# Attention and mixture block on one core: first stores on two queues, early projections in other banks, 69 unused products on TensorE

## The reference

```python
x = x + tanh(g_xattn[0]) * attention(layernorm(x), ctx_512)      # x: 8 x 256 x 128, ctx: 8 x 256 x 64
x = x + tanh(g_ffn[0]) * experts(layernorm(x))
# attention(x, c), 16 heads of 8 numbers
q, k, v = x @ Wq + bq, x @ Wk + bk, x @ Wv + bv
y = softmax(causal(q k^T / sqrt(8))) @ v
qc, kc, vc = x @ Wcq + bcq, c @ Wck + bck, c @ Wcv + bcv
y = y + softmax(qc kc^T / sqrt(8)) @ vc
return y @ Wp + bp
# experts(x): 16 experts of width 64, 2 of 4 groups and 4 experts chosen for each token
out = sum_e combine[:, e] * ((silu(x @ w_gate[e].T) * (x @ w_up[e].T)) @ w_down[e].T)
```

## Time and profile before

| | us |
|---|---|
| median of 3 runs | 352.14 (351.76 to 352.70) |
| the profiled execution, its own time | 352.36 |
| its span, first to last instruction | 350.6 |

### The profile page before, as it was taken

The page is one execution under the profiler, slowest core; times in us unless marked ns, Lnnn a source line. Parts: engine busy times, 40 slices in busy tenths (PEclk is TensorE's granted clock), DMA queues, the critical chain, the costliest instruction groups (busy, mean ns, idle before and its releaser), DMA issues.

```text
span 350.6 us, 8629 instructions
## 1 busy us (share of the span) xinstructions
PE 324.8 (93%) x3186; PEld 250.0 (71%) x3186; DVE 255.3 (73%) x639; ACT 196.1 (56%) x399; POOL 151.6 (43%) x174
## 2 busy tenths in 40 slices
PE   2577899999999999899999999999999999996896
PEld 1343474576687788678888789777978887774765
DVE  3325784777887888988889888787889965658642
ACT  2332244757876875586567656675756656542041
POOL 4783315203470169427743725286400461714222
PEclk9999999999999999999999999999999999999899
DMA  4547677577637686268647852366434203214000
GB/s 122 98 120 185 156 185 140 153 195 160 220 92 175 121 155 151 70 146 160 142 112 128 195 135 69 85 127 161 120 83 103 39 17 89 38 50 87 11 6 15
DMA packets 32890, 40.45 MB, mean 115 GB/s; under 512 B 3441, under 2 KB 29825, under 8 KB 30369
## 3 DMA queue, kind: packets, MB, share of 16 engines
q1 hardware_dynamic: 32848, 39.91, 49.6%
HBM read 29.84 MB, written 7.45 MB: 106 GB/s over the span
## 4 chain that ended last, share of the span: by engine, by line
PE 82%; DVE 7%; issue 2%; DMA 2%; ACT 2%; POOL 2%; SPq 2%; DVEq 0%; POOLq 0%; ACTq 0%
PE bank L891 15%; PE bank L825 15%; PE bank L782 9%; PE bank L804 8%; PE bank L779 7%; PE bank L912 7%; PE bank L801 6%; PE bank L845 3%; DVE row_max L978 2%; PE bank L866 2%; PE bank L831 2%; PE bank L861 1%; PE bank L925 1%; PE bank L852 1%; PE bank L847 1%
## 5 line engine op out<-in xcount | busy, mean ns | idle before, releaser
L978 DVE TENSOR_REDUCE row_max<-bank 128x2 f32<-128x512 f32 (+1 forms) x224 | 147.3, 686 | 45.5 <-PE bank L782 29.7
L694 ACT ACTIVATE probs<-bank 128x512 f32<-128x512 f32 x224 | 126.4, 595 | 55.3 <-PE bank L804 30.4
L891 PE MATMUL bank<-xn2T,w_pairs_sb 128*128 128x256 f32 x256 | 67.3, 387 | 1.2 <-DVE f_gate L1058 0.6
L825 PE MATMUL bank<-probs,v_ext 128*32 128x256 f32 (+1 forms) x1024 | 56.8, 363 | 0.0
L618 POOL TENSOR_TENSOR f_h<-f_h,comb 128x512 f32<-128x512 f32 x32 | 40.2, 1270 | 33.9 <-DMA comb<-c_scr 14.3
L782 PE MATMUL bank<-k_stack,q_stack 72*128 72x256 bf16 x256 | 50.8, 295 | 3.5 <-DMA k_stack<-k_scr 2.1
L891 PEld LDWEIGHTS bank<-xn2T,w_pairs_sb 128*128 128x128 f32 x256 | 43.7, 190 | 8.2 <-issue 3.1
L804 PE MATMUL bank<-q_stack,k_stack 73*128 73x256 bf16 x256 | 46.5, 285 | 0.2
L825 PEld LDWEIGHTS bank<-probs,v_ext 128*32 128x32 f32 x1024 | 29.8, 111 | 20.0 <-issue 3.4
L407 POOL TENSOR_TENSOR rest<-proj,part 128x512 f32<-128x512 f32 x14 | 16.2, 1159 | 54.7 <-ACT part L667 54.7
L779 PE MATMUL bank<-k_stack,q_stack 121*128 121x128 bf16 (+1 forms) x384 | 38.7, 231 | 0.3 <-DVE row_max L978 0.2
(11 more groups left out here) (113 smaller groups left out, 388.6 us busy)
## 6 DMA issues: line engine op xcount, KB each, us to landing
q_stack<-q_scr SPq DMA_DIRECT2D x15, 576.0 KB
k_stack<-k_scr SPq DMA_DIRECT2D x45, 192.0 KB
comb<-c_scr SPq DMA_DIRECT2D x14, 512.0 KB, 7.1
q_scr<-part SPq DMA_DIRECT2D x48, 64.0 KB
k_scr<-part SPq DMA_DIRECT2D x48, 64.0 KB
x_in<-in_x SPq DMA_DIRECT2D x8, 128.0 KB, 2.5
w_pairs_sb<-in_w_pairs SPq DMA_DIRECT2D x1, 1024.0 KB, 5.2
out<-y_out SPq DMA_DIRECT2D x8, 128.0 KB, 1.9
```

The source lines that it names most:

```text
L694: nc.scalar.activation(probs[:, seq % NP, :], exp_bank[s % 2][:, :], ACT.Exp).then_inc(exp_done, 1)
L825: last = pe.matmul(pv_bank[32 * n:32 * n + VW, col + q0:col + T], v[:, VW // 2 * odd:VW // 2 * odd + VW], weights, start=odd == 0 and kt = ...
L891: last = pe.matmul(bank_of[:, n * T:(n + 1) * T], w[:, e0:e0 + 128], xn2T[:, :], start=True, stop=True)
L978: nc.vector.tensor_reduce(row_max[:, kind, qt, h0:h0 + nh], max_bank[k % 2][:, :].rearrange("p (h k) -> p h k", h=nh), AX.X, ALU.max).then ...
```

## The change

**Stores and loads of element 0.** The functions `store_part`, `load_rows`, `load_stack` and `load_first` take the engine as an argument, and ACT issues five of the words that SP issued: `pd0:0`, `pd0:0:1`, `qh:0`, `qh:0:1` and `qst:0:1`. Each part has its own semaphore `part_out[kind][n]`, which counts two DMAs of an element.

**Projections of elements 0 to 2** (`EARLY = 3`) go to `gate_bank` (cross) and `up_bank` (self) instead of `misc`, with semaphores of their own. The first gates and ups wait until the last of them is copied out.

**`keep_busy`**: a product of the identity with itself, float32, 128 by 128, into `pv_bank`, whose result nothing reads. It waits for nothing, and PE's list has the word `warm:0` for it 69 times, all of them ahead of `exp:0:5`: 13 after `vproj:0`, 6 after `xnT:1`, 19 ahead of `max:0`, and 31 between the chunks `max:0` to `max:0:22`.

**`vclear`** clears the two halves of `v_ext` in two words, and waits for the cross parts of element 0 instead of for its normalised x.

**All five orders are written anew.** Other words than those named are the same, in another order; the first 60 or so of each engine differ most.

```diff
+EARLY = 3
+MISC_USES = [word for word in order("pe") if word[0] in MISC and not (word[0] == "proj" and word[1] < EARLY)]
...
-        part_out = [sem("part_out_cross"), sem("part_out_self")]
+        part_out = [[sem(f"part{n}_out_{kind}") for n in range(PARTS)] for kind in ("cross", "self")]
...
+        def store_part(eng, b, kind, n):
+            eng.wait_ge(split[kind], b * PARTS + n + 1)
+            if n == 0:
+                stack_here(eng, b - 2, kind)
+            q, k = part[:, kind, n, 0:T], part[:, kind, n, T:2 * T]
+            eng.dma_start(q_scr[b % 2, kind, n].rearrange("d h x -> (d h) x"), q).then_inc(part_out[kind][n], 16)
+            eng.dma_start(k_scr[b % 2, kind, :, n], k).then_inc(part_out[kind][n], 16)
...
+        def load_first(eng, qk, half):
+            for n in range(PARTS):
+                eng.wait_ge(part_out[CROSS][n], 32)
+            heads = slice(half * H // 2, (half + 1) * H // 2)
+            load_rows(eng, qk, 0, CROSS, heads, stack_in[0][CROSS] if half else first_heads_in)
...
-            def clear_values():
-                pool.wait_ge(xn_done, 1)
-                v = v_ext[:, :, :, :, :, :].rearrange("p a k n e v -> p (a k n) e v")
+            def clear_values(parity):
+                pool.wait_ge(split[CROSS], PARTS)
+                v = v_ext[:, parity].rearrange("p k n e v -> p (k n) e v")
...
             def project(b, kind):
-                misc_filled(act, "proj", b, kind)
+                src, done = (misc, misc_free) if b >= EARLY else ((gate_bank, up_bank)[kind], proj_free[kind])
+                if b < EARLY:
+                    act.wait_ge(proj_ready[kind], b + 1)
+                else:
+                    misc_filled(act, "proj", b, kind)
...
             def values(b):
                 misc_filled(act, "vproj", b)
-                act.wait_ge(v_cleared, 1)
+                act.wait_ge(v_cleared, b % 2 + 1)
...
+                elif what == "pd0":
+                    store_part(act, b, n, 0)
+                elif what == "qh":
+                    load_first(act, 0, n)
+                elif what == "qst":
+                    load_stack(act, b, n, 0)
...
+            def project_early(b, n):
+                ge(pe, proj_free[n], b)
+                project(b, n, (gate_bank, up_bank)[n]).then_inc(proj_ready[n], 1)
...
+            def keep_busy():
+                pe.matmul(pv_bank[:, 0:128], ident[:, :], ident[:, :], start=True, stop=True)
```

393 lines of the change are left out of this document (202 added, 191 removed).

## The result

| | before | after |
|---|---|---|
| median of 20 runs each, us | 351.56 (349.58 to 354.01) | 349.64 (346.85 to 355.36) |
| the profiled execution, its own time | 352.36 | 346.85 |
| its span | 350.6 | 345.1 |

The ratio is 0.9939, with a 95% interval of 0.9915 to 0.9962: the change makes the kernel faster by 0.6%, about 2 us. Forecast were 342.2 us and 338 to 349. The median lies above that range. Two further measurements of the same kernel (`again`, `again2`) gave 0.9923 and 0.9908. An execution more than 1.5% above the fastest of its kernel is left out of a ratio, but not out of a median or a range.

The account below looks back on a forecast made before the run. PE was taken to set the long rest, with PE waiting in a fill up to about 50 us; 4.0 + 3.5 + 3.4 - 1.0 = 9.9 us gave 342.2 us against the median, range 338 to 349.

Parts of the forecast that it names:

- the marker: Start of max:1:4, just behind pv:0, where both kernels are compared: 59.73 us before, forecast at 49 to 50.
- Part 1: Fill up to the first scores: first stack earlier, scores start at 25.0 instead of 28.98 us, gain 4.0 us.
- The second queue: Element 0's stores on ACT too: worth only two issues of 0.58 us that SP no longer makes, about 1.2 us.
- The two banks: Early projections: proj:0:1 follows proj:0 without waiting for its copy, about 1 us on a waiting chain, nothing more.
- The rival in which the clock falls in the stretch of maxima: Clock not kept while DVE sets the pace: in full 353 to 369 us, chance 0.05.
- Part 2: First scores to max:1: DVE's maxima take 20.2 us, PE's 19.2 fit beside; 23.7 before, gain 3.5 us.
- Part 3: From max:1 to the start of max:1:4, at full clock: 3.7 us instead of 7.1, gain 3.4 us.
- part 4: Taken back: the same bytes in less time delay one of the stacks by 0 to 3 us; 1 taken.
- `max:1` at 45: Sign expected in the changed kernel's trace: max:1 starts at 45 us, 52.66 before.
- Rest behind the marker: nothing: From max:1:4 to the end: same work at the same clock, 291 us as before, so no gain or loss.
- the second rival: Clock not kept, since PE stops for its banks: in part 345 to 351 us, 0.06; in full 353 to 369, 0.05.
- the first rival: First heads or masks land 4 us later than placed, eating the fill's gain: about 346 us, chance 0.14.

Follow-up runs that it names:

- one_queue: Changed kernel with the five words ACT issues given back to SP, each ahead of its neighbour of the same kind: 350.11 us, 0.9948.
- no_warm: Changed kernel without its 69 unused products, all else equal: 353.87 us, 1.0035.
- bridge: Changed kernel plus 12 unused products in gate_bank, 6 ahead of max:1 and 6 between the chunks that follow: 348.79 us, 0.9897.
- bridge2: The changed kernel with 12 further unused products around max:1, measured again in another job: 344.99 to 352.70 us beside one outlying execution, 0.9850.
- zero_shift: Changed kernel with zeros for the maxima's rows of elements 0 and 1, so SP needn't wait for them, those words moved: 346.29 us, 0.9840.
- zero_shift_bridge: Changed kernel with zeros for the maxima of elements 0 and 1, without SP's wait, plus 12 further unused products around max:1: 345.93 us, 0.9807.
- one_bank: Changed kernel with projections of elements 0 to 2 back in misc (EARLY = 0), those of elements 1 and 2 ordered cross, self: 353.91 us, 1.0076.
- shift_act: Changed kernel with the small transfers of the maxima of elements 0 and 1 issued by ACT behind its own copies, not SP: 358.43 us, 1.0182.
- zero_early_bridge: Changed kernel, zeros for elements 0 and 1's maxima placed early, element 1's loads right behind their stores, 12 further unused products: 346.99 us, 0.9875.

## Why the forecast was wrong

**The forecast said** that the marker would gain 4.0 + 3.5 + 3.4 = 10.9 us, that 1 us would be lost again at a stack, and nothing behind the marker. In the profile the marker gained 59.73 - 53.21 = 6.5 us and the rest lost 345.1 - 53.21 = 291.9 against 290.9, 1.0 us. The sum is 5.5 instead of 9.9.

| stretch, us | forecast | measured |
|---|---|---|
| to the first scores | 25.0 | 24.7 |
| from there to `pv:0` | 20.2 | 22.4 |
| `pv:0` to the marker | 3.7, and the 1.0 for a stack | 6.1 |
| the rest | 290.9 | 291.9 |

**Part 1 was right**, 4.3 us for 4.0, in the order that was given: PE comes to `max:0` straight from an unused product, without a wait, at 24.71 (25.0). But two things in it were priced wrongly without harm to the sum. The second queue gives nothing that shows (`one_queue`). The two banks, at "about 1 us" and "nothing more", carry more: without them, and with the unused products as they are, the start is at 27.83 and the time 1.4 to 1.7% longer. The sum went along PE's new order, in which the copies are no longer waited for, and so it contained the banks' share without naming it.

**The clock was right up to `pv:0`.** It rises early and holds through the stretch of maxima, 1.93 us for `pv:0`. That the products are "there only to raise the clock" is not what they do here: the kernel's own float32 products raise it, and the unused ones hold it (`no_warm`). The rival in which the clock falls in the stretch of maxima did not come.

**Part 2 failed first, by 2.2 us**, in "It fits, with 1.0 us to spare". DVE is busy for 18.4 us from 24.71 to 47.67, where its last row maximum ends (45.2 by the sum). The rest it waits, and the two long waits are for PE's own work:

```profile
31.00 0.69 DVE L1023 TENSOR_REDUCE row_max<-bank 128x2 f32<-128x512 f32 x1 [1.59 <-PE bank L809]
...
40.13 1.89 DVE L1023 TENSOR_REDUCE row_max<-bank 128x4 f32<-128x512 f32 x3 [1.94 <-PE bank L806]
```

```profile
38.59 1.28 PE L968 MATMUL bank<-ident 128*128 128x128 f32 x10
```

In the first PE is at the values of element 1 and three unused products, in the second at the projection of element 2, a transpose and six unused products, five of them in this row. PE has no wait for a transfer in either. Both sums of work were about right, but PE's comes in lumps, DVE is fed by two banks only, and a lump longer than they bridge is lost. So some of the unused products stood in DVE's way after all; a run with fewer of them there was not made.

**Part 3** had 3.7 us and the stretch took 6.1. The wait for the key stack is 1.16 us of it, which part 4 had allowed for, and waits for VectorE and ScalarE are 0.6. In the changed order `pv:0` stands ahead of `max:1`, not behind four chunks of it, so the sign "`max:1` at 45" could not have come even by the sum; and of the four `exp` chunks that were counted at nothing one more stands in this stretch.

**The step that failed in its reason is part 4**, "between 0 and 3 us of delay at one of the stacks; I take 1". It divided bytes by the best rate over the whole stretch. PE waited not at one stack but at three, 1.16, 0.78 and 1.68 us, together 3.6 us for 1 (4.2 and 5.6 in the other two profiles), and at the first of them for another reason: it is the end of a chain, from the third part (32.3 us) over a store that lands 5 to 6 us after its issue, or a transfer that must go first, to a load that needs 7 to 8 us. Both prices were 2.2 and 3.9 us in the rows I used, from moments at which less was in flight. The DMA engines even stand idle for part of that chain: from 40.0 to 42.8 us they moved 29 GB/s. That a mean rate leaves room says nothing on a chain of store, landing and load. DVE idles for 3.3 us there, but `pv:0` stands in most of that; at PE, which does the work in order, the stack costs 1.2.

**"Rest behind the marker: nothing"** failed in its reason. The prediction said it would be wrong "because the head start runs into something that comes at its own time", and it is: the stacks at `max:2` and at 127 us come at their own time too. The head start is 8.3 us at `pv:0`, 8.0 at `pv:0:1`, 6.9 and 6.3 at the two that follow, and 3.8 at `pv:1` (80.83 against 84.62); part of this decline is order, since the changed kernel has done 15 chunks of `exp` at the marker and the old one 11. From `pv:1` to the end the two kernels take 264.3 and 266.0 us. That is luck in part: the old profile has a fall of the clock near 326 us in it, worth 1.7 us.

**From the profile to the median** another 3.6 us are lost (0.8 of them because the old profile lies above its own median). The time over the clock in the 20 runs shows where: the profiled execution ran at 0.995, the median one at 0.985 to 0.990. In the profiles of the changed kernel the fall was seen behind the wait for the stack, 3.3 and 7 us long, and filling that stretch with products takes it away in the profile of `bridge`, though not in that of `bridge2`. That is the second rival, in part, and one element later than I had it: between the chunks of element 0 the unused products hold the clock, and they end at `max:0:22`; between those of element 1, where VectorE and ScalarE set the same pace and the stack adds a wait, there are none. I gave it 0.06, and the first rival, late transfers, 0.14. Both happened, and neither is merely a consequence of the other: `zero_shift` took the wait away and not the fall, `bridge` the fall and not the waits, and the two together (`zero_shift_bridge`) gave the lowest ratio of all, 0.9807, though the intervals of these three overlap. How much of the 3.6 us is the clock and how much the transfers, which also differ from execution to execution, isn't separated.

**What is not settled.** What fewer unused products among the chunks of element 0, or behind `vproj:0` with one bank, would give was not run. How the store's landing and SP's wait would behave if both were taken away together with the masks was not run. No run here issues the loads for element 1 before 40 us with the small transfers in time. And the fall of the clock was seen in profiles only; that the slower of the other runs have longer or further falls is inferred from their mean clock.

## What to carry to other kernels

When a change gives an engine a head start, don't subtract it from the end: go through the transfers that the engine will meet, and write for each when it can be issued and by what chain (last part ready, store landed, queue free), with landing times taken from rows at the same traffic. A transfer that stood just in time before is the new bound, and a gap that opens there can cost the clock as well. Products that nobody reads are worth placing in such waits, where they cost little, but alone they gained nothing here, and where the wait goes they stand in the way (2.5 us in `one_bank`, 1.15 in `zero_shift_bridge`); when two engines' sums of work fit beside each other, look also at the longest lump of one of them; and a small transfer that someone waits for is better issued ahead of large ones, on whatever queue.

## What the runs showed of the hardware

- **A small transfer behind large ones.** 8 KB that land 2.2 us after issue in a quiet moment took 8.6 and 8.7 us behind 0.8 MB and more (`shift_act`), on another queue than the large ones, and 6.9 us in `again2`, on the same queue. The 8 KB row of zeros of the changed kernel took 12.25 us from 114.93 on, with a DMA share of 0.95 to 1.02 from 112 to 124 us. Stores of 64 KB took 4.9 us (`zero_shift`) and 6.0 us (`zero_early_bridge`), issued at DMA shares of 0.86 and 0.90.
- **The clock and what precedes it.** In the changed kernel it rose at 10.4 us, under float32 instructions that follow each other almost without a gap from 7.7 us on. In other profiles of the same sequence it rose as late as 13 to 14 us (`bridge`, whose 26 unused products from 13.09 us on take 3.42 us instead of 3.07), so the moment isn't tied to a product; in `one_bank`, with two waits of about 1 us in the stream, it rose behind 15.7 us, under the unused products. It fell at about 55 us behind 6 us in which PE was busy for 3.8, and at about 17 us in `no_warm`, behind a wait of 3.4 us. In the profile of `bridge`, whose 12 further products stand in the first of these stretches, it doesn't fall; in that of `bridge2`, the same kernel with a wait of 1.95 us there, it falls at about 54 us.
- **A third level.** One execution of `bridge2`, of some 250 of all kernels, took 1554 us. Its stretches:

```profile
85.00:100.00 15.00, 14.95 (x41) 7.23 (x42) 4.14 (x7) 3.07 (x7) 6.66 (x6) 0.20 0.55 157
...
150.00:1550.00 1400.00, 1399.16 (x2566) 907.69 (x2564) 198.02 (x518) 159.46 (x304) 107.52 (x113) 0.16 0.08 18
```

From about 86 us to the end the column reads 0.16, with PE busy all the time. The other profiles show half and full only. Ahead of it PE had longer waits than in `bridge`, 1.95 us at `max:1` and 2.19 us at 81 us, each with a fall to half clock behind it, as other profiles have them too; it did not come again, so its cause stays open; a median of many runs is not moved by it, a mean would be.
